# A two-layer attention and mixture-of-experts kernel: a changed expert loop in layer two, and norm, choice and join of the layers in parts

## What is computed

```python
x = _layernorm(x + _L0_attn_ref(x, ...))   # rope, softmax attention
x = _layernorm(x + _L0_ffn_ref(x, ...))    # each of 8 experts takes the 256 tokens that it rates highest
x = _layernorm(x + _L1_attn_ref(x, ...))   # keys and values from a latent of 32
x = _layernorm(x + _L1_ffn_ref(x, ...))    # each token takes its best 4 of 16 experts

# layer one's experts
route_vals, routes = jax.lax.top_k(softmax(xf @ Ws + bs).T, 256)
out = (gelu(xf[routes] @ W1 + b1) @ W2 + b2) * route_vals[..., None]
final = jnp.zeros((N, D)).at[routes.reshape(-1)].add(out.reshape(-1, D))

# layer two's experts
logits = -sum((x[:, :, None, :] - keys) ** 2) + x @ rw.T + rb
topv, topi = jax.lax.top_k(logits, 4)
fused = sum(softmax(topv)[..., None] * exp_out_of_expert[topi], axis=2)
```

## Time and profile before

| | us |
|---|---|
| median of three runs (831.3 to 836.78) | 834.6 |
| the profiled execution's own time | 832.95 |
| span from its first to its last instruction | 831.1 |
| busy in the span: PE, DVE, ACT, POOL | 593.2, 478.9, 486.8, 400.2 |

### The profile page before, as it was taken

One profiled execution on the slowest core, in us unless ns is written; L12 is line 12 of the kernel. 1 busy time (PEld: TensorE's weight loads), 2 busy tenths in 40 slices (PEclk: granted clock), 3 DMA queues, 4 the chain that ended last, 5 costly groups with the idle time before them and its releaser, 6 DMA issues.

```text
span 831.1 us, 17381 instructions
## 1 busy us (share of the span) xinstructions
PE 593.2 (71%) x4619; PEld 401.6 (48%) x4620; DVE 478.9 (58%) x1801; ACT 486.8 (59%) x1207; POOL 400.2 (48%) x511
## 2 busy tenths in 40 slices
PE   3699999975028654899999996287777777777670
PEld 1244444434017643345444445176666666666660
DVE  4877878824664326658888843854444444444415
ACT  1277777762008733357777775076767667667751
POOL 3955553000017842222223201068888888888860
PEclk9999999995559986569999996589999999999985
DMA  5410810001002350720300001023233233333244
GB/s 158 126 60 7 237 42 1 1 2 51 0 10 37 45 121 6 216 90 26 108 1 0 2 1 52 7 39 45 40 43 44 40 43 44 40 43 44 40 68 118
DMA packets 68641, 43.63 MB, mean 52 GB/s; under 512 B 15798, under 2 KB 62191, under 8 KB 68594
## 3 DMA queue, kind: packets, MB, share of 16 engines
q1 hardware_dynamic: 51698, 29.73, 12.5%
q0 software_dynamic: 16896, 13.32, 12.0%
HBM read 27.22 MB, written 14.23 MB: 50 GB/s over the span
## 4 chain that ended last, share of the span: by engine, by line
PE 32%; DVE 20%; issue 17%; DMA 13%; POOL 13%; ACT 3%; DVEq 1%; POOLq 0%; ACTq 0%; SPq 0%
DMA sum<-rt,idx_s 10%; PE bank L624 7%; POOL prob L574 7%; PE bank L640 5%; PE bank L657 5%; DVE mx L1155 5%; POOL sum L578 3%; POOL hold L571 3%; DVE KB L1196 2%; DMA Y<-sum 2%; PE bank L805 2%; DVE passed L1280 2%; PE bank L774 2%; DMA prob<-xs,idx_g 1%; PE bank L768 1%
## 5 line engine op out<-in xcount | busy, mean ns | idle before, releaser
L1155 DVE TENSOR_REDUCE mx<-bank 128x2 f32<-128x512 f32 x256 | 170.2, 688 | 58.5 <-PE bank L624 55.6
L992 ACT ACTIVATE prob<-bank 128x512 f32<-128x512 f32 x256 | 145.9, 602 | 40.7 <-PE bank L640 37.0
L578 POOL DMA_INDIRECT sum<-rt,idx_s x96 | 152.8, 1592 | 28.7 <-issue 21.4
L1083 ACT ACTIVATE prob<-bank,prob 128x128 f32<-128x128 f32 x384 | 109.8, 370 | 54.3 <-PE bank L886 54.0
L571 POOL TENSOR_TENSOR hold<-ones 128x1 f32<-128x1 f32 x106 | 71.7, 677 | 120.4 <-DVE idx_g L1424 116.5
L624 PE MATMUL bank<-KB,QT 128*128 128x512 f16 x256 | 104.0, 413 | 23.2 <-DVE mx L1155 16.0
L1414 DVE TENSOR_SCALAR_CACHE_REDUCE hit<-bank,slot_at 128x128 f32<-128x128 f32 x96 | 39.9, 416 | 124.3 <-PE bank L895 124.3
L905 PE MATMUL bank<-W,prob 128*128 x768 | 107.9, 284 | 1.5 <-ACT prob L1083 0.9
L886 PE MATMUL bank<-rt,prob 128*128 128x128 f32 x768 | 107.6, 285 | 0.0
L574 POOL DMA_INDIRECT prob<-xs,idx_g x96 | 96.0, 1000 | 16.5 <-issue 14.2
L886 PEld LDWEIGHTS bank<-rt,prob 128*128 128x128 f32 x768 | 97.1, 198 | 1.5
(11 more groups left out here) (239 smaller groups left out, 929.0 us busy)
## 6 DMA issues: line engine op xcount, KB each, us to landing
W<-in_w SPq DMA_DIRECT2D x48, 256.0 KB, 3.5
sum<-zero SPq DMA_DIRECT2D x4, 1088.0 KB, 8.1
xs<-X SPq DMA_DIRECT2D x2, 1024.0 KB, 5.3
XB<-sum SPq DMA_DIRECT2D x8, 256.0 KB, 4.9
xr<-XT SPq DMA_DIRECT2D x12, 128.0 KB, 2.1
prob<-xs,idx_g POOLq DMA_INDIRECT x96, 2.6
sum<-rt,idx_s POOLq DMA_INDIRECT x96
out<-X SPq DMA_DIRECT2D x2, 512.0 KB, 3.7
```

The costliest lines, as they stand in the source:

```text
L578: nc.gpsimd.indirect_dma_start(sums_d[lay][(s - 1) % 2], bass.IndirectOffsetOnAxis(idx_s[:, (s - 1) % 4:(s - 1) % 4 + 1], 0), yo[:, (s - 1 ...
L992: nc.scalar.activation(prob[:, v % 8, :, :], st_bank(i - 1, v)[:, :], ACT.Exp, scale=SCALE).then_inc(exp_done, 1)
L1083: last = nc.scalar.activation(hid[:, s % 2, f, :], bank[2 + s % 2][:, P * f:P * f + P], (ACT.Gelu_apprx_tanh, ACT.Gelu)[lay], bias=wc[:, s ...
L1155: nc.vector.tensor_reduce(m_at, bank[S1B[u % 2]][:, :].rearrange("p (j k) -> p j k", j=2), AX.X, ALU.max).then_inc(s1_used, 1)
```

## The change

1. *Layer two's scatter.* Each selected row gets a place of its own in a scratch `parts` of 4 x 2,048 rows: number of the choice (by expert) times 2,048 plus the token's row. So nothing is added by the DMA. POOL works the places out once (`place_of_each_choice`), and they are gathered along with gates (rows of 160 instead of 144 floats). The four slices are read back by SP and added by DVE and POOL; the first three are read as soon as their experts are through (`count_tiles`, `choices_in`).
2. *The loop's skew.* Lists 5 and 6 ahead of the tile, gather 4 ahead, transpose 2 ahead (1 before), second product 2 behind (1 before), scaling 3 and scatter 4 behind. The buffers `xsT`, `hid` are four deep, `gcol`, `idx_s` eight. `hold` goes; a semaphore increment (`slot_open`) stands before each indirect DMA. The copies of first weights go from ACT to SP's DMA queue in layer two (`expert_in`), and in layer one they go altogether: its tiles' experts are known when the program is written.
3. *Layer one's scatter.* Three sums, by expert; the first two experts' tiles and the last one's are written without addition. The token's row there is `16 p + t`, so that sums are read with 8 KB a partition. Biases are added by one more matmul a tile. Padding steps of the slot table go.
4. *Norm and choice beside the last batch.* Tiles 0 to 11, then 12 and 13, then 14 and 15 are normed, turned and rated in iterations 8 and 9. POOL makes the scale as a power of -0.5 and norms 8 tiles; the square root on ACT goes.
5. *Join in chunks of four tiles*, at both layers' ends: addition, statistics, scale (POOL), norm (two tiles DVE, two ACT), turn, and the output's DMA by chunks.

```diff
             def pool_slots(lay, j, s):
...
-                wait_for(pool, held, (NJT[0] + AHEAD + 1) * lay + j + (AHEAD if isinstance(j, int) else AHEAD - 3))
-                nc.gpsimd.tensor_tensor(hold[:, s:s + 1], ones[:, 0:1], ones[:, 0:1], ALU.mult).then_inc(held, 1)
...
+                k = j + NJT[0] * lay
+                if is_tile(lay, j + 4):
+                    pool.wait_ge(idx_ready, k + 5)
+                    pool.sem_inc(slot_open)
+                    gather(lay, s % 4)
+                if is_tile(lay, j - 4):
+                    pool.wait_ge(yo_ready, k - 3)
+                    q, slot, here = (s - 4) % 8, yo[:, s % 4, :], scattered[s % 4]
+                    if lay == 0 and j % 2 == 0:
+                        landed(pool, k - 7, (s - 7) % 4)
+                    pool.sem_inc(slot_open)
+                    to = bass.IndirectOffsetOnAxis(idx_s[:, q:q + 1], 0)
+                    if lay == 1:
+                        nc.gpsimd.indirect_dma_start(d["parts"], to, slot, None).then_inc(here, 16)
+                    elif 4 <= j - 4 < NJT[0] - 2:
+                        nc.gpsimd.indirect_dma_start(sums_d[sum_buffer(j - 4)], to, slot, None,
+                                                     compute_op=ALU.add).then_inc(here, 16)
+                    else:
+                        nc.gpsimd.indirect_dma_start(sums_d[sum_buffer(j - 4)], to, slot, None).then_inc(here, 16)
...
+            def expert_in(t, s):
+                e = tile_expert(sp, 1, t, 0, s, sp_experts)
+                if not (isinstance(t, int) and t < 4):
+                    sp.wait_ge(gelu_done, t + NJT[0] - 3)
+                sp.dma_start(wc[:, s, :], W[:, bass.ds(e, 1), 0:W2AT].rearrange("p a f -> p (a f)")).then_inc(wc_in[s], 16)
...
             def pe_slots(lay, j, s):
+                if is_tile(lay, j + 2):
+                    q = (s + 2) % 4
+                    pe.wait_ge(gathered[q], 4 * (k + 2 - q) + 16)
+                    wait_for(pe, xsT_ready, k + 1)
+                    nc.tensor.transpose(slot_bank(0, q), xg[:, q, 0:P], ident[:, :]).then_inc(tp_done, 1)
...
+                    if lay == 1:
+                        pe.wait_ge(wc_in[s % 4], 4 * (j - s % 4) + 16)
...
             def act_slots(lay, j, s):
-                    e = tile_expert(act, lay, ej_in, j + 4, s, act_experts)
-                    nc.scalar.copy(wc[:, (s + 2) % 4, :], W[:, bass.ds(e, 1), 0:W2AT]).then_inc(wc_ready, 1)
...
+            def scale(n):
+                t0, t1 = norm_tiles(n)
+                pool.wait_ge(var_ready, n + 1)
+                nc.gpsimd.tensor_scalar(mv[:, t0:t1, 1], mv[:, t0:t1, 1], EPS, None, ALU.add).then_inc(rstd_ready, 1)
+                pool.wait_ge(rstd_ready, n + 1)
+                nc.gpsimd.tensor_tensor(rstd[:, t0:t1], mv[:, t0:t1, 1], mhalf[:, t0:t1], ALU.pow).then_inc(scale_ready, 1)
...
+            def tail_normalise(lay):
+                scale(7 * lay)
+                pool.wait_ge(scale_ready, 7 * lay + 1)
+                for c in (1, 2):
+                    for t in range(4 * c, 4 * c + 4):
+                        last = nc.gpsimd.tensor_scalar(X[:, t, :], Y[:, t, :], mv[:, t, 0:1], rstd[:, t:t + 1],
+                                                       ALU.subtract, ALU.mult)
+                    last.then_inc(tail_pool, 1)
...
+            def tail_before(lay, i, u):
+                if i == NB and u == 0:
+                    tail_scale(lay, 0)
...
+                if i == NB + 1 and u == 4:
+                    tail_evac(lay, 3)
+                    if lay == 0:
+                        soft_logits(0)
+                    else:
+                        choice_scores(0)
...
+            def join_chunk(n):
+                at, t0 = slice(4 * (n % 4), 4 * (n % 4) + 4), 4 * (n % 4)
+                for t in range(t0, t0 + 4):
+                    last = nc.vector.bn_stats(stats[:, t, :], Y[:, t, :])
+                step(last)
+                for t in range(t0, t0 + 4):
+                    last = nc.vector.bn_aggr(mv[:, t, :], stats[:, t, :])
+                last.then_inc(var_ready, 1)
+                dve.wait_ge(scale_ready, join_group(n) + 1)
+                for t in range(t0, t0 + 2):
+                    last = nc.vector.tensor_scalar(X[:, t, :], Y[:, t, :], mv[:, t, 0:1], rstd[:, t:t + 1],
+                                                   ALU.subtract, ALU.mult)
+                last.then_inc(join_dve, 1)
...
                 else:
+                    join_turn(0)
+                    pe.wait_ge(join_xt, 1)
                     front_latent(lay, 0, 0)
+                    join_turn(1)
+                    front_proj(lay, 0, 0, 0)
+                    join_turn(2)
+                    front_proj(lay, 0, 0, 1)
+                    join_turn(3)
+                    query_transposes(lay, 0, 0)
+                    pe.wait_ge(join_xt, 3)
+                    key_transposes(lay, 0, 0)
+                    front_latent(lay, 1, 1)
+                    front_proj(lay, 1, 1, 0)
+                    front_proj(lay, 1, 1, 1)
...
+            def choices_joined():
+                for c in range(4):
+                    at = slice(4 * c, 4 * c + 4)
+                    pool.wait_ge(part_ready, c + 1)
+                    pool.wait_ge(end_back[c], 16)
+                    nc.gpsimd.tensor_tensor(Y[:, at, :], X[:, at, :], slice_of[TOPK - 1][:, at, :],
+                                            ALU.add).then_inc(last_slice, 1)
+                    if c > 0:
+                        scale_and_shift(join_group(4 + c - 1))
+                scale_and_shift(join_group(7))
```

More of the change, by code:

```diff
@@ L714, in pe_iteration @@
                         last.then_inc(pj_done, 1)
+                    if isinstance(i, int) and i >= NB:
+                        tail_turns(lay, i, u)
                     if u in (7, 8) and soft_on:
@@ new lines, in tail_logits @@
+            def tail_logits(lay, n):
+                t0, t1 = TURN[n]
+                w, E = (ws0, wr1)[lay], (E0, E1)[lay]
+                pe.wait_ge(xt_ready, 5 * lay + n + 1)
+                for t in range(t0, t1):
+                    out, at = (bank[M5], E * t) if n < 3 else (bank[2], E * (t - EARLY))
+                    last = nc.tensor.matmul(out[:, at:at + E], XT[:, P * t:P * t + P], w[:, :], start=True, stop=True)
+                if n in (2, 4):
+                    last.then_inc(lg_done, 1)
@@ new lines, in tail_turns @@
+            def tail_turns(lay, i, u):
+                if i == NB:
+                    if u == 2 and lay == 1:
+                        pe.wait_ge(wr_ready, 2)
+                        nc.tensor.matmul(bank[M6][:, 0:E1], ones[:, :], ksq[:, :], start=True,
+                                         stop=True).then_inc(ksq_done, 1)
+                    if u == 7:
+                        pe.wait_ge(tq2_ready, 2 * (NB - 1 + NB * lay) + 2)
+                        tail_turn(lay, 0)
+                    if u == 10:
+                        tail_logits(lay, 0)
+                        tail_turn(lay, 1)
+                    if u == 13:
+                        tail_logits(lay, 1)
+                        tail_turn(lay, 2)
+                else:
+                    if u == 2:
+                        tail_logits(lay, 2)
+                        tail_turn(lay, 3)
+                    if u == 4:
+                        tail_logits(lay, 3)
@@ L823, in gate_bias, with join_turn @@
+            def join_turn(c):
+                wait_for(pe, join_xt, c - 1)
+                pe.wait_ge(join_dve, c + 1)
+                for t in range(4):
+                    if t == 2:
+                        pe.wait_ge(join_act, c + 1)
+                    last = nc.tensor.transpose(bank[6 + c % 2][:, P * t:P * t + P], X[:, 4 * c + t, :], ident[:, :])
+                last.then_inc(join_turned, 1)
             def gate_bias(lay, E):
-                pe.wait_ge(gate_ready, lay + 1)
+                pe.wait_ge(gate_ready, 2)
@@ L1061, in turn_evac, with join_normalise @@
-            def turn_evac(n):
-                for c in range(0, 4, 2):
-                    act.wait_ge(xt_done, 4 * n + c + 1)
-                    nc.scalar.copy(XT[:, CH * c:CH * c + CH], bank[c][:, :]).then_inc(xt_act, 1)
+            def join_normalise(n):
+                act.wait_ge(neg_ready, 2 * n + 2)
+                for t in range(4 * (n % 4) + 2, 4 * (n % 4) + 4):
+                    last = nc.scalar.activation(X[:, t, :], Y[:, t, :], ACT.Identity, bias=nmr[:, t:t + 1],
+                                                scale=rstd[:, t:t + 1])
+                last.then_inc(join_act, 1)
@@ L1433, in _ @@
+                if lay == 1 and isinstance(j, int) and j == 3:
+                    count_tiles()
             nc.vector.memset(selz[:, 0:1], 0.0)
```

860 lines of the change are left out of this document (516 added, 344 removed).

## The result

On record the changed kernel took 855.63 us, median of 4 runs (853.75 to 858.83), and the kernel before 833.92 beside it: ratio 1.026, interval [1.022, 1.031]. It is slower by 2.6%; I had said 752.5 in a range of 720 to 796, with 0.04 for slower. That number is one of two that this program has. The same unchanged kernel ran three times more, each time on another chip: 774.58 us (ratio 0.931 [0.926, 0.935]), 856.25 (1.027 [1.021, 1.032]) and 775.18 (0.929 [0.926, 0.932]). The kernel before takes 833 to 835 on all of them, and kernels whose POOL issues its DMAs as fast as this one, run beside each other on one chip, agreed in which kind of chip it was. So there are two questions: what costs 80 us on some chips, and why even the other chips give 774.6 and not 752.5.

What follows compares the result with a forecast made beforehand. No one engine bounded the whole kernel; POOL's own instructions bounded layer two's loop. Savings of 45 + 5 + 7 + 2 + 6.5 + 8.5 + 8 = 82 us took 832.95 to 751, adjusted to 752.5; range 720 to 796.

Steps and rivals of the forecast that it cites:

- layer one's loop: Layer one's expert tiles: known experts, no weight copy, six plain scatters, 52.5 us against 57.5, -5; -2 if those stay 1.6.
- layer two's loop: Layer two's 80 expert tiles: POOL's period falls from 3.28 to 2.65 us, 222 us against 267.3, -45.
- slow rival: Layer two's loop: SP's weight copies set the pace; at 4.2 us a copy the kernel takes 864; chance 0.04.
- Rival one: Layer two's loop: the writing scatter stays at 1.6 us, saving 6 instead of 45, total 791; chance 0.20.
- Rival two: Layer two's loop: POOL's gaps shrink and PE sets 2.25 us a tile, total 723; chance 0.13.
- Norm and choice: After attention's last Y: most work moves beside the last batch, -8.5 in layer two and -7 in layer one.
- charge of 3: Layer two's norm and choice: 3 us charged for DVE's scores and max of 12 tiles ahead of the last norm.
- sign of being wrong: Attention's last batch: expected 2 to 3 us longer; the forecast is wrong if its tail grows by over 5 us.
- charge of 2: Layer one's norm and choice: 2 us (0 to 6) charged for the work moved beside the last batches.
- Rival three: Norm and choice: hidden work holds up the last batch, both gains go, +16, total 768; chance 0.10.
- The join: Between the layers: sums read early, last one in chunks of 3.5 us, first score at +27.5, -6.5 (-12 to +3).
- The end: After layer two's last scatter: three slices added early, the last in chunks, 17 us against 25.1, -8 (-11 to 0).

Runs made afterwards that it cites:

- a0_after: The changed kernel, unedited, run again on another chip, one with on-time semaphores: 774.58 us.
- p1_before_plain: The kernel before with one edit, layer two's scatters write instead of adding: 853.19 us, ratio 1.026.
- a1_after: The changed kernel, unedited, run once more, on a chip with late semaphores: 856.25 us, ratio 1.027.
- k1: The changed kernel with layer two's scatter adding again, onto rows of parts that SP set to zero: 827.38 us, ratio 0.990.
- f3: The changed kernel with batch 1's front moved earlier at the join and the end's last slices added by DVE, statistics ahead of norm: 764.76 us, ratio 0.918.
- e1: The changed kernel with a one-element POOL multiply before each gather in both expert loops: 778.96 us; on a late-semaphore chip 855.59.

## Why the prediction was wrong, and where it was right

The account by stages, from first gathers and last scatters of the traces (record and a0_after, each less before); the first column is what I had said.

| stage | forecast | record | a0_after |
|---|---|---|---|
| layer one up to its first gather | -9 | -6.7 | -5.5 |
| layer one's loop | -5 | +3.7 | -4.7 |
| from there to layer two's first gather | -15 | -1.0 | -4.0 |
| layer two's loop | -45 | +27.1 | -49.0 |
| end | -8 | +2.8 | +2.6 |
| sum | -82 | +25.9 | -60.6 |

**Layer two's loop, as recorded: the step that failed.** I wrote that "POOL's own instructions are the bound of this loop" and took every microsecond off them as one off the loop. What the runs showed in its place: in the record's runs and on two of the five chips of the experiments a gather and a scatter in 2.57 to 2.68 us make the semaphores of PE come late to ACT and DVE, and the loop takes 291 to 297 us. The floor lies between 3.0 and 3.2 us, measured on one of these chips; below it the loop gets slower than it was. The kernel before stood at 3.28, just above, so nothing in its trace could show it; none of my rivals had it. My slow rival, the weight copies, has the wrong mechanism: on a chip with on-time semaphores half or a thirty-second of the bytes leaves loop two at 218.8 and 218.3 us, and on one with late ones p1_before_plain is slow without any copy. Its price of 864 came close by accident. The 72 us between -45 and +27.1 are seven tenths of the 103 us by which I missed; layer one's loop, which has late semaphores too, is 9 more there (4 in a1_after).

**The same step where semaphores are on time: right.** Window of a0_after over layer two's loop, and two steps of POOL:

```profile
524.40:742.90 218.50, 187.15 (x1559) 174.18 (x1560) 119.97 (x642) 133.31 (x485) 159.15 (x160) 0.98 0.50 165
```
```profile
640.39 0.97 POOL L700 DMA_INDIRECT prob<-xs,idx_g  x1 [0.30 <-issue]
641.67 0.99 POOL L719 DMA_INDIRECT parts<-rt,idx_s  x1 [0.30 <-issue]
642.96 0.97 POOL L700 DMA_INDIRECT prob<-xs,idx_g  x1 [0.30 <-issue]
```

Period 2.57 for my 2.65 (the 0.05 for increments is nothing), 218.5 for my 222, and layer one's loop -4.7 for -5. Rival one (scatter stays 1.6) is false on every chip, and with it goes the reading that I gave to the Trainium skill's DMA: Bandwidth & Descriptors (Anatomy of one DMA, SWDGE path), that an addition's extra descriptors cost POOL nothing. The pages of the profiles have 8,544 packets in POOL's queue for after and 17,504 for k1, whose 80 scatters add: 112 packets and 0.6 us more for each. The Trainium skill's GPSIMD Engine Reference (Key points) has POOL contend with some instructions of DVE, and my estimate from it was a period of 2.8; that didn't come: DVE is busy 120 us of this loop and POOL's instructions keep 0.97 and 0.99. Rival two (PE sets 2.25) didn't come: PE is busy 187 of 218.5 us, but the 0.30 gaps stayed in every tile.

**Norm and choice: right behind the last Y, wrong ahead of it.** In a0_after layer two's last Y is at 502.68 and the table's first matmul at 515.23, 12.5 us where I said about 12. The charge of 3 for work ahead of the last norm was too small. The last Y and the one two batches before it, in the kernel before and then in a0_after:

```profile
482.52 0.42 DVE L1162 TENSOR_TENSOR Y<-bank,XB 128x256 f32<-128x256 f32 x1
...
506.75 0.42 DVE L1162 TENSOR_TENSOR Y<-bank,XB 128x256 f32<-128x256 f32 x1 [2.12 <-PE bank L712]
```
```profile
471.97 0.41 DVE L1414 TENSOR_TENSOR Y<-bank,XB 128x256 f32<-128x256 f32 x1
...
502.68 0.42 DVE L1414 TENSOR_TENSOR Y<-bank,XB 128x256 f32<-128x256 f32 x1 [1.28 <-PE bank L896]
```

The two batches take 30.7 us where they took 24.2: 6.5 for my 3, and past the 5 that I had named as a sign of being wrong. The same 30.6 to 30.7 stands in the record and in every run whose code for it is that of after, on chips of both kinds. The whole stretch from first score to last Y hides it (172.8, before 170.6), since a0_after's attention began at a granted clock of 0.66 over 34 us and the kernel before's at 0.57; the record, at the same clock as before, has 177.0. So of the 8.5 that I had forecast layer two keeps 3.7, and 4.2 of a0_after's shorter stretch are the clock. Layer one's last two batches take 27.8, before 24.3 (3.5 for a charge of 2), and the stretch behind them is 9.6 shorter (49.0 to the first gather, before 58.6) for 11. Rival three was thus true in part: the hidden work does hold up the last batch, but doesn't eat the whole gain.

**The join: failed, +3.9 for -6.5.** Timeline of a0_after:

```profile
292.73 0.33 SPq L565 DMA_DIRECT2D Y<-sum  x1
...
297.69 2.29 DVE L1681 TENSOR_TENSOR X<-X,Y 128x2048 f32<-128x2048 f32 x1 [3.42 <-DMA Y<-sum]
300.01 0.69 DVE L1685 TENSOR_TENSOR Y<-X,W 128x512 f32<-128x512 f32 x1
...
304.04 0.69 DVE L1685 TENSOR_TENSOR Y<-X,W 128x512 f32<-128x512 f32 x1
...
327.78 0.79 PE L958 MATMUL bank<-wq,XT 128*128 128x128 f32 x2
...
329.87 1.04 PE L808 MATMUL bank<-KB,QT 128*128 128x512 f16 x2
```

Three terms were short. "Two of three sums are read and added under the last tiles": one of them waits for a scatter two tiles before the end, is issued at 292.73 and added until 299.98, so the first chunk starts 7.9 us behind the last scatter where I had 3. A chunk takes 4.0, not 3.5. And batch 1's front stands between the keys and the first score; I knew of it and gave it nothing beyond 3.5, f3 got 2.7 of it back.

**The end: failed, +2.6 for -8.** POOL's groups of a0_after and two chunks:

```profile
L678 POOL TENSOR_SCALAR X<-Y,mv,rstd 128x128 f32<-128x128 f32 x16 | 12.8, 810 | 0.2
L660 POOL TENSOR_TENSOR rstd<-mv,mhalf 128x4 f32<-128x4 f32 x8 | 8.3, 1038 | 0.7
L749 POOL TENSOR_TENSOR Y<-X,KB 128x512 f32<-128x512 f32 x4 | 5.0, 1260 | 5.2 <-DMA KB<-parts 5.2
L660 POOL TENSOR_TENSOR rstd<-mv,mhalf 128x12 f32<-128x12 f32 x2 | 4.6, 2297 | 0.2
```
```profile
752.83 1.26 POOL L749 TENSOR_TENSOR Y<-X,KB 128x512 f32<-128x512 f32 x1
...
756.18 1.26 POOL L749 TENSOR_TENSOR Y<-X,KB 128x512 f32<-128x512 f32 x1
```

The chunks come every 3.35 us, a serial ring of POOL's add, DVE's statistics and POOL's power, and the first starts at 748.14, 5.2 behind the last scatter. I had summed POOL's work alone (10 us for four chunks; it is 13.4) and put the power at 0.4. It is 0.72 for 2 columns, 1.04 for 4 and 2.30 for 12; the last two are outside my bounds of 0.2 to 0.85, which I had taken from other instructions. That f3 got 2.9 us by breaking the ring, with the power unchanged, shows the ring; the price of the power alone wasn't tried. (My sum for POOL in layer one's loop was also off: its terms give 51.7, not 52.5.)

What brings the late semaphores stays open. Shown is that the pace of indirect DMAs decides, and that transfers aren't short of room: the DMA share is 0.36 in the record's slow loop and 0.50 in a0_after's fast one, and p1_before_plain, as slow, has 0.14 in 560 to 740. One rival of e1's expectation, that the supply of instructions stops, was given no run of its own. The traces speak against a wait for their transfer. The queues that bring instructions, in 560 to 800 of the record's loop:

```profile
q8 instruction: 2, 0.03, 0.0%
q14 instruction: 2, 0.02, 0.0%
```

Four packets in 240 us, and a0_after has as many in 560 to 740. The Trainium skill's SBUF — State Buffer (Who interferes with whom) has one rule, that only the port pair of DVE and GpSimd contends. ACT stands here for 6.6 us beside DVE's 3.8, so that rule doesn't cover it. Whether it is the chip itself or where a program lies on it, five chips can't tell.

## What to carry to other kernels

Where one engine issues DMAs in an unbroken string, its instructions' durations aren't the whole price: before speeding such a string up, look whether the trace of before has ever run at the new pace, and if not, give a floor a chance of its own. Two edits that cure the same stall are a sign that something else did: run the unchanged kernel beside them. Sum a chunked tail as a ring through all its engines, not as the work of the busiest. And measure a charge where it falls (here the last two batches), not over a whole stage in which the granted clock can differ by more than the charge.

## What the runs showed of the hardware that I had not expected

- On some chips a gather and a scatter of 128 rows of 512 to 640 bytes, issued by POOL in 3.0 us or less, make a loop of 80 tiles 20 us and more longer than the 267 of the kernel before, and semaphores that ACT and DVE wait for rise late, by up to 5.5 us in the stretch shown; on others 2.57 us is free. The kernel before, at 3.28, takes 833 to 835 us on both kinds.
- An indirect scatter with addition takes POOL 1.57 to 1.61 us and 112 more packets in its queue than one without, which takes 1.03; the gather takes 0.97.
- POOL's power costs 0.72 us for 2 columns and 2.30 for 12: some 0.16 a column. A one-element multiply between two indirect DMAs costs 0.1 us beyond the gap that is there anyway.
- SP moved 258 KB into each tile's slot, some 97 of the 165 GB/s of the loop (worked out from 80 copies in 218.5 us), at no measurable cost (774.58 against 770.13 with half, ranges overlapping).
- The same attention of layer two took 191.8, 194.6 and 198.7 us by the granted clock of its first 34 us (0.84, 0.66, 0.57), in executions that agree in the code of that stretch.
